# Graph network on one core: three spherical chunks copied over the rows by DMA, both small weight layers in fp32 on two row halves, edge features loaded once

## The reference, cut to what matters

```python
wk = relu(edge_features @ k_w1 + k_b1) @ k_w2 + k_b2      # [E, 128], the same with v_ for wv
acc = sh[:, 0:1] * (x_dst @ C[:, 0, :])                   # tensor_product: S = 9 spherical numbers
for s in range(1, S):
    acc = acc + sh[:, s:s+1] * (x_dst @ C[:, s, :])
k = (acc with Cqk) * wk                                   # and v = (acc with Cv) * wv
attn = einsum('ehd,ehd->eh', q[edge_src], k)              # then a softmax over the edges of a node
upd  = segment_sum(v * alpha)                             # and the weighted sum of the values
```

## Time and profile before

| | us |
|---|---|
| median of 3 runs | 2949.27 |
| profiled execution, its own time | 2947.53 |
| its span | 2945.7 |
| TensorE busy in the span | 2469.1 |
| VectorE | 2612.7 |
| GpSimd | 1731.3 |
| ScalarE | 1514.6 |

### The profile page before, as it was taken

One profiled execution on the slowest core, in us unless ns is written; L12 is line 12 of the kernel. 1 busy time (PEld: TensorE's weight loads), 2 busy tenths in 40 slices (PEclk: granted clock), 3 DMA queues, 4 the chain that ended last, 5 costly groups with the idle time before them and its releaser, 6 DMA issues.

```text
span 2945.7 us, 48186 instructions
## 1 busy us (share of the span) xinstructions
PE 2469.1 (84%) x12310; PEld 1787.3 (61%) x12505; DVE 2612.7 (89%) x3389; ACT 1514.6 (51%) x2914; POOL 1731.3 (59%) x1719
## 2 busy tenths in 40 slices
PE   2233347999999999999999999999999999999714
PEld 1233315677777776777677776777677777777511
DVE  6688835899999999999999999999999999999737
ACT  1321224566666655666566665666566566666310
POOL 1800037777777766667676666666666677665030
PEclk7555557999999999999999999999999999999855
DMA  6787714245555544444444444444445544544340
GB/s 187 202 222 187 210 25 111 76 131 149 148 149 145 148 147 139 141 142 148 139 144 142 146 147 140 140 144 147 142 141 147 148 141 142 148 144 132 121 124 11
DMA packets 282407, 415.35 MB, mean 141 GB/s; under 512 B 64463, under 2 KB 191875, under 8 KB 278470
## 3 DMA queue, kind: packets, MB, share of 16 engines
q1 hardware_dynamic: 222278, 296.67, 32.4%
q0 software_dynamic: 52704, 107.19, 15.1%
q10 hardware_dynamic: 7128, 8.13, 0.8%
HBM read 309.59 MB, written 102.20 MB: 140 GB/s over the span
## 4 chain that ended last, share of the span: by engine, by line
PE 52%; DVE 7%; issue 6%; ACT 3%; DMA 2%; POOL 2%; SPq 0%; DVEq 0%; ACTq 0%; POOLq 0%
PE bank L1118 11%; PE bank L1120 9%; PE bank L1119 9%; PE bank L1142 5%; PE bank L1163 4%; PE bank L1194 2%; PE bank L1124 2%; PE bank L1125 2%; PE bank L1095 2%; PE bank L1113 2%; DVE xa_t L1538 1%; DVE z_l L1546 1%; PE bank L1102 1%; POOL gathered L745 1%; PE bank L1101 1%
## 5 line engine op out<-in xcount | busy, mean ns | idle before, releaser
L745 POOL DMA_INDIRECT gathered<-xtab_d,src_g x784 | 780.6, 996 | 449.7 <-PE bank L1095 203.0
L745 POOL DMA_INDIRECT gathered<-qtab_d,dst_g x784 | 801.9, 1023 | 257.2 <-issue 249.0
L1118 PE MATMUL bank<-z_h,wt_h 128*128 128x512 f32 x1568 | 729.6, 465 | 27.9 <-DVE val L1578 27.9
L1538 DVE TENSOR_TENSOR xa_t<-bank,r_r 128x512 f32<-128x512 f32 x980 | 667.3, 683 | 13.5 <-PE bank L1142 10.3
L876 ACT ACTIVATE z_h<-xa_t 128x512 fp32r<-128x512 f32 x980 | 617.4, 634 | 110.1 <-DVE xa_t L1538 100.3
L1120 PE MATMUL bank<-z_h,wt_l 128*128 128x512 f32 x1568 | 620.7, 396 | 0.0
L1119 PE MATMUL bank<-z_l,wt_h 128*128 128x512 f32 x1568 | 618.8, 395 | 0.0
L1546 DVE TENSOR_TENSOR z_l<-xa_t,z_h 128x1024 fp32r<-128x1024 f32 x392 | 478.0, 1219 | 48.2 <-ACT z_h L876 44.6
L1118 PEld LDWEIGHTS bank<-z_h,wt_h 128*128 128x128 f32 x1568 | 301.1, 192 | 131.4 <-issue 92.7
L869 ACT ACTIVATE hid<-bank,b1kv 128x512 f32<-128x512 f32 x196 | 134.8, 688 | 476.4 <-PE bank L1102 462.4
L1120 PEld LDWEIGHTS bank<-z_h,wt_l 128*128 128x128 f32 x1568 | 294.9, 188 | 69.2
(11 more groups left out here) (222 smaller groups left out, 4057.9 us busy)
## 6 DMA issues: line engine op xcount, KB each, us to landing
nrow_d<-x_r SPq DMA_DIRECT2D x196, 288.0 KB
ea<-in_ea_t SPq DMA_DIRECT2D x392, 128.0 KB
exb<-exd_d SPq DMA_DIRECT2D x392, 128.0 KB
dmb<-exd_d SPq DMA_DIRECT2D x392, 128.0 KB
ea_c<-in_ea_t SPq DMA_DIRECT2D x49, 512.0 KB, 5.0
aggrow_d<-xa_t SPq DMA_DIRECT2D x49, 512.0 KB, 3.9
gathered<-xtab_d,src_g POOLq DMA_INDIRECT x784
gathered<-qtab_d,dst_g POOLq DMA_INDIRECT x784
```

Of the source, the lines that this page charges most:

```text
L745: rows_in = pool.indirect_dma_start(rows[:, c % 4, k, :], None, table, bass.IndirectOffsetOnAxis(ap=picked[:, s, at:at + 1], axis=0))
L1118: pe.matmul(ps[:, :], wt_h[rows, w, :], high, start=start, stop=False)
L1538: dve.tensor_tensor(z[:, i, :], bank[2 + (NJ * c + i) % 2][:, :], xt[:, c % 2, :], ALU.mult).then_inc(z_ok, 1)
```

## The change

Chunks 0 and 1 stay as they are (NS = 2); the numbers of chunks 2, 3 and 4 come straight from HBM in fp32 by three DMAs of a group, `load_harmonics`, with semaphores of their own (`sh_b_in`). VectorE multiplies these three chunks in one instruction, ScalarE rounds them in one, so `z_ok` counts NZ = 3 a group. Both small layers use plain fp32 matmuls without a split. The edge features of a group are loaded once: columns 0 to 255 on partitions 0 to 63 and 256 to 511 on 64 to 127. `hidden` has one matmul of 256 columns for each half, into banks 2 and 3; it is moved a group ahead and behind `weights`. `weights` has four of 256 columns, in turns on partitions 0 to 63 and 64 to 127.

```diff
             def load_edge(j, c):
-                past(sp, eal_ok, j, c, 2)
+                past(sp, hid_ps, j, c, 2, 2)
                 hold()
                 for half in range(2):
-                    sp.dma_start(ea2[half * D:(half + 1) * D, c % 2, :], edges_t[:, bass.ds(group(j, c) * G, G)]
-                                 ).then_inc(ea_in[c % 2], 16)
+                    sp.dma_start(ea2[half * D:(half + 1) * D, c % 2, :],
+                                 columns(edges_t, j, c)[:, half * HG:(half + 1) * HG]).then_inc(ea_in[c % 2], 16)
...
+            def load_harmonics(j, c):
+                past(sp, z_ok, j, c, 2, NZ)
+                hold()
+                for i in range(NS, NJ):
+                    k = 2 * i
+                    rows = columns(harmonics_t[k:min(k + 2, S), :], j, c)
+                    n = min(2, S - k)
+                    sp.dma_start(sh_b[:, c % 2, i - NS, :], rows.rearrange("s (o w) -> s o w", o=1)
+                                 .to_broadcast([n, P // n, G])).then_inc(sh_b_in[c % 2], 16)
...
             def body(j, c):
+                if live(j, c + 2):
+                    load_harmonics(j, c + 2)
                 if live(j, c + 3):
                     load_edge(j, c + 3)
...
             def front_h(j, c):
-                done(act, hid_ps, j, c)
+                done(act, hid_ps, j, c, 2)
+                past(act, wk_ps, j, c, 1)
                 past(act, wv_ps, j, c, 1)
-                act.activation(hid[:, :], ps_hw[:, :], ACT.Relu, bias=b1kv[:, :]).then_inc(hid_ok, 1)
-                act.activation(hid_h[:, :], ps_hw[:, :], ACT.Relu, bias=b1kv[:, :]).then_inc(hid_ok, 1)
+                for f in range(2):
+                    act.activation(hid[:, f * HG:(f + 1) * HG], bank[2 + f][:, 0:HG], ACT.Relu, bias=b1kv[:, :]
+                                   ).then_inc(hid_ok, 1)
...
             def hidden(j, c):
-                done(pe, eal_ok, j, c)
-                past(pe, wv_ok, j, c, 1)
-                pe.matmul(ps_hw[:, :], wt_h[:, W1KV, :], ea_hl[:, c % 2, :], start=True, stop=False)
-                pe.matmul(ps_hw[:, :], wt_l[:, W1KV, :], ea_hl[:, c % 2, :], start=False, stop=True
-                          ).then_inc(hid_ps, 1)
+                landed(pe, ea_in, j, c, 32)
+                if not isinstance(j, int) or c >= 1:
+                    done(pe, z_ok, j, c - 1, NZ, NS - NZ)
+                for f in range(2):
+                    half = slice(f * D, (f + 1) * D)
+                    pe.matmul(bank[2 + f][:, 0:HG], w1kv[half, :], ea2[half, c % 2, :], start=True, stop=True
+                              ).then_inc(hid_ps, 1)
...
-                for ps, rows, done_ps in ((ps_xw, slice(0, D), wk_ps), (ps_hw, slice(D, P), wv_ps)):
-                    split_matmul(ps, W2KV, hid_h[rows, :], hid_l[rows, :], True, True, rows).then_inc(done_ps, 1)
+                for f in range(2):
+                    edges = slice(f * HG, (f + 1) * HG)
+                    mk = pe.matmul(ps_xw[:, edges], w2kv[0:D, :], hid[0:D, edges], start=True, stop=True)
+                    mv = pe.matmul(ps_hw[:, edges], w2kv[D:P, :], hid[D:P, edges], start=True, stop=True)
+                mk.then_inc(wk_ps, 1)
+                mv.then_inc(wv_ps, 1)
...
             def outer(j, c, i):
...
+                if i < NS:
+                    done(dve, shb_ps, j, c, NS, i + 1 - NS)
+                    dve.tensor_tensor(z[:, i, :], bank[2 + i][:, :], xt[:, c % 2, :], ALU.mult).then_inc(z_ok, 1)
+                else:
+                    landed(dve, sh_b_in, j, c, 16 * (NJ - NS))
+                    dve.tensor_tensor(z[:, NS:NJ, :], sh_b[:, c % 2, :, :],
+                                      xt[:, c % 2, :].rearrange("p (o g) -> p o g", o=1)
+                                      .to_broadcast([P, NJ - NS, G]), ALU.mult).then_inc(z_ok, 1)
```

More of the change, by code:

```diff
@@ L27 @@
 NJ = 5
-CK, CV, W2KV, W1KV = 0, NJ, 2 * NJ, 2 * NJ + 1
-NW = 2 * NJ + 2
+CK, CV, CEND = 0, NJ, 2 * NJ
+NW = CEND
+NS = 2
+NZ = 3
 H = 8
@@ L102, in gnn_two_layers @@
         wt_l = sb("wt_l", [P, NW, O], F32R)
+        w1kv = sb("w1kv", [P, O])
+        w2kv = sb("w2kv", [P, O])
         head_sel = sb("head_sel", [P, 2 * BP - H])
@@ L350, in gnn_two_layers @@
         qg_in = [sem(f"qg_in{i}") for i in range(2)]
-        eah_ok = sem("eah_ok")
-        eal_ok = sem("eal_ok")
+        sh_b_in = [sem(f"sh_b_in{i}") for i in range(2)]
         batch_in = sem("batch_in")
@@ L507, in arrived, with columns, loads_and_stores @@
                 eng.wait_ge(ring[b], (g - b + n) * (per // n))
-        def loads_and_stores(sp, edges_t):
+        def columns(m, j, c):
+            turn, at = divmod(c, UNROLL)
+            by_turn = m.rearrange("d (n u w) -> d n u w", u=UNROLL, w=G)
+            if isinstance(j, int):
+                return by_turn[:, turn, at, :]
+            return by_turn[:, bass.ds(j + turn, 1), at, :].rearrange("d o w -> d (o w)")
+        def loads_and_stores(sp, edges_t, harmonics_t):
             sp.dma_start(x_r[:, :, 0:D], a["x"].rearrange("(t p) d -> p t d", p=P)).then_inc(x_in, 16)
@@ L590, in load_edge @@
                 hold()
-                sp.dma_start(s3[0:SP3, c % 4, :], sh3_d.rearrange("a s e -> (a s) e")[:, bass.ds(group(j, c) * G, G)]
-                             ).then_inc(s3_in[c % 2], 16)
+                sp.dma_start(s3[0:SP3, c % 4, :], columns(sh3_d.rearrange("a s e -> (a s) e"), j, c)).then_inc(s3_in[c % 2], 16)
+            def load_harmonics(j, c):
[7 more added lines that the diff above has]
+                                 .to_broadcast([n, P // n, G])).then_inc(sh_b_in[c % 2], 16)
             def store_exponents(j, s):
@@ L615, in store_row @@
                 hold()
-                sp.dma_start(nrow_d[bass.ds(group(j, c) * G, G), :].rearrange("(p j) w -> p (j w)", p=P),
+                turn, at = divmod(c, UNROLL)
+                to = nrow_d.rearrange("(n u p k) w -> n u p (k w)", u=UNROLL, p=P, k=4)
+                to = to[turn, at] if isinstance(j, int) else \
+                    to[bass.ds(j + turn, 1), at].rearrange("o p w -> (o p) w")
+                sp.dma_start(to,
                              row[:, c % 2, :, :].rearrange("p j w -> p (j w)")).then_inc(row_out[c % 2], 16)
             def body(j, c):
+                if live(j, c + 2):
+                    load_harmonics(j, c + 2)
                 if live(j, c + 3):
@@ L874, in outer_high @@
                     past(act, acc_ps, j, c, 2)
-                done(act, z_ok, j, c, NJ, i + 1 - NJ)
-                act.activation(z_h[:, c % 2, i, :], z[:, i, :], ACT.Copy).then_inc(zh_ok, 1)
+                done(act, z_ok, j, c, NZ, i + 1 - NZ)
+                chunks = slice(i, i + 1) if i < NS else slice(NS, NJ)
+                act.activation(z_h[:, c % 2, chunks, :], z[:, chunks, :], ACT.Copy).then_inc(zh_ok, 1)
             def front_q(j, c):
@@ L1083, in _ @@
             pe.wait_ge(sel_done, 1)
-            pe.wait_ge(wtl_padded, 3)
+            pe.wait_ge(wtl_padded, 2)
             pe.wait_ge(head_ok, 2)
@@ L1139, in spread @@
                     landed(pe, s3_in, j, c)
-                if not isinstance(j, int) or c * NJ + i >= 2:
-                    done(pe, z_ok, j, c, NJ, i - 1 - NJ)
-                pe.matmul(bank[2 + (NJ * c + i) % 2][:, :], sel[:, i, :], s3[:, c % 4, :], start=True, stop=True
-                          ).then_inc(shb_ps, 1)
+                    done(pe, hid_ok, j, c, 2)
+                pe.matmul(bank[2 + i][:, :], sel[:, i, :], s3[:, c % 4, :], start=True, stop=True).then_inc(shb_ps, 1)
             def products(j, c, i):
@@ L1199, in body @@
                 if live(j, c + 1):
-                    spread(j, c + 1, 0)
-                    spread(j, c + 1, 1)
+                    for i in range(NS):
+                        spread(j, c + 1, i)
                 if live(j, c + 2):
@@ L1206, in body @@
                 if live(j, c + 1):
-                    hidden(j, c + 1)
                     q_turn(j, c + 1)
@@ L1211, in body @@
                         products(j, c, i)
-                    if i + 2 < NJ and live(j, c + 1):
-                        spread(j, c + 1, i + 2)
                     if i == 1 and live(j, c + 1):
                         weights(j, c + 1)
+                    if i == 1 and live(j, c + 2):
+                        hidden(j, c + 2)
                     s = batch_at(c, 10)
@@ L1367, in _ @@
             dve.wait_ge(wtl_ok, 1)
-            for w in (CK + 4, CV + 4, W1KV):
+            for w in (CK + 4, CV + 4):
                 dve.memset(wt_l[D:P, w, :].bitcast(F32), 0.0).then_inc(wtl_padded, 1)
@@ L1628, in body @@
                     outer(j, c + 1, 1)
-                    hidden_low(j, c + 1)
+                    outer(j, c + 1, 2)
+                    outer_low(j, c + 1, 0)
                 if live(j, c - LAG):
                     sum_values(j, c - LAG)
-                if live(j, c + 1):
-                    outer_low(j, c + 1, 0)
-                    outer(j, c + 1, 2)
```

(6 more changed lines are left out.)

57 lines of the change are left out of this document (18 added, 39 removed).

## The result

The changed kernel takes 4099.07 us (median of 4 runs, 4096.1 to 4104.68) against 2949.32 (4 runs, 2947.16 to 2950.45) for the kernel before on the same chip: ratio 1.390, 95% interval 1.388 to 1.393. The forecast was 4130 us, slower.

What follows compares the result with a forecast made beforehand. It took two DMA engines, carrying the copies with two source rows, as the bound: 184 x 18.0 + 12 x 14.3 = 3484 us replaces the loop's 2300, so 2949 - 2300 + 3484 = 4133, about 4130 us; range 3800 to 4500.

Steps and rivals of the forecast that it cites:

- Two engines for a pair copy, 18.0 us a group: Copies of chunks 2 and 3: two source rows mean two DMA engines, 408 KB each, 18.0 us a group.
- The sum: Whole kernel: 184 groups at 18.0 us and 12 at 14.3 make 3484 us for 2300, rest unchanged, 4133 us.
- VectorE waits at the product of three chunks, some 7 us a group: Sign on VectorE: it would wait for a DMA at the three-chunk product, some 7 us a group.
- DMA share some 0.4: Sign in the profile: share falls to some 0.4 though bytes rise by nearly two fifths, as most engines idle.
- The exponents' copies queue behind: DMA queue: the exponents' copies would wait behind the copies on the two engines, which need 11.5 us a group.
- Issuing them is no matter: SyncE's queue: issuing the three added DMAs takes 0.63 us each, 1.9 us more a body, and doesn't matter.
- Passes side by side, 1.58 us for the added block; TensorE 10.85 us: TensorE: six fp32 half-row matmuls in three slots of 0.43 plus 0.29, 1.58 us; body 11.43 - 2.16 + 1.58 = 10.85.
- Clock mixed, TensorE within the 18 us: TensorE's clock: expected mixed, its work still inside 18 us a group; the clock as the bound had 0.03.
- VectorE's work, 10.0 us a group: VectorE: from 11.3 us a group, less two dropped instructions and some 0.1 from the fused product, to 10.0.
- By the row GpSimd stays at 10.1 us: GpSimd's gathers: unslowed beside VectorE instructions with two SBUF inputs, 10.1 us a group; by the skill's rule up to 11.9.
- the wide rival: DMA copies spread over eight or more engines: TensorE sets the pace, 10.9 us a group, 2800 us; chance 0.09.
- the other side of the forecast: Whole kernel faster, about 2800 us, if the copies spread wide; faster by over 0.2% had chance 0.09.

Runs made afterwards that it cites:

- e1_wide: The changed kernel with each copy of chunks 2 and 3 cut into two DMAs of one source row, same bytes: 3096.66 us, ratio 1.050.
- e9_six: e1_wide with three gathers where four are, TensorE turning the third tile twice: 2789.54 us, ratio 0.947.
- e7_weights: The kernel before with only the second small layer in plain fp32, four matmuls of 256 columns on two row halves: 2959.92 us, ratio 1.005.
- e5_thirds: e1_wide with the three-chunk product cut into three one-chunk instructions that follow each other at the same place: 2925.57 us, ratio 0.992.
- e11_cuts: e5_thirds with the two z_l instructions of 1024 columns cut into four of 512: 2844.89 us, ratio 0.965.
- e2_half: The changed kernel with the copy of chunk 2 alone cut into two DMAs of one source row: 3274.92 us, ratio 1.112.
- e3_four: The changed kernel with chunks 2 and 3 each copied from four source rows to 32 partitions: 3177.76 us (one run).

## Why the prediction was right, and where it was not

- **Two engines for a pair copy, 18.0 us a group.** Right, the mechanism too: 17.8 us once exponents and rows are there, and 14.1 for the twelve groups before, where the sum had 18.0 and 14.3. By the 408 KB of the busiest engine that is 408 / 17.8 = 22.9 KB/us, where I took 22.8 from the best slice. Two engines show in the DMA share of 0.13, in the increments that come late and in their number. `e1_wide` shows that it is the shape of the copy and not its bytes: 1002 us less with the same bytes.
- **The sum.** The loop came out at 3421 us and not 3484, 63 less; what lies outside it came out at 4099 - 3421 = 678 us and not 649, 29 more, of which 17 lie ahead of the first spread (476.5 for 459.4 us). The sum took this part as unchanged, and why it grew wasn't followed. The two misses partly cancel, so that 4133 stands as near to 4099 as it does is in part luck.
- **VectorE waits at the product of three chunks, some 7 us a group.** Right, 6.7. **DMA share some 0.4.** Right, 0.42.
- **The exponents' copies queue behind.** Right in kind: what lies behind the pair copies on the two engines is late. The page of waits shows it at the edge features, for which TensorE waits 4.4 us a group. "Issuing them is no matter" was wrong: three issues took 9.35 us. No run shows that this cost time of its own, and none rules it out; the 18.0 us of the two engines account for the whole without it.
- **Passes side by side, 1.58 us for the added block; TensorE 10.85 us.** Right: 1.59 us for the block and 10.88 us a body in `e9_six`, 1.15 for the four matmuls of `weights` alone in `e7_weights`.
- **Clock mixed, TensorE within the 18 us.** Right: 0.83 granted, with TensorE busy 225 of 300 us.
- **VectorE's work, 10.0 us a group.** Near: 269 of 300 us in `e9_six`, 9.8 a group. Three products of 682 ns against one of 1756 are 0.29 us less by these rows, not the 0.1 of the text; nothing hangs on it.
- **The step that failed: "By the row GpSimd stays at 10.1 us".** In the earlier trace rows the gather had begun 0.16 us before the VectorE instruction, so it wasn't the one to wait. The rows of `e1_wide` with the other order show the hold, and so do rows of the kernel before. Worked out from `e1_wide`, gathers cost (1.24 - 1.00) x 8 = 1.9 us more a group, close to the "up to 1.8" that I wrote down from the Trainium skill's rule (GPSIMD Engine Reference, 8. Key points) and then set aside. In the changed kernel this lies under the copies' 17.8 us and costs nothing; but the wide rival was priced at 2800 us, and with the change as written it is 3097. So the other side of the forecast, faster with 0.09, needed more than wide copies: it needed the product cut as well (`e5_thirds`, `e11_cuts`).

What stays open: what part of `e2_half` and `e3_four` beyond the count of engines belongs to the held gathers; what the stopped queue costs by itself; and why the part outside the loop grew by 29 us.

## What to carry to other kernels

Before a DMA that fans a few rows out to many partitions, count its source rows: with two of them a copy ran on two of 16 engines, and the same bytes as two DMAs of one row each took a quarter off the kernel's time. A DMA share that falls while the bytes rise is how it looks in a profile, and two increments of another DMA that come late, behind 14 in time, show it directly. Where GpSimd's instructions stand near the bound, the length of VectorE's instructions with two SBUF inputs counts, not only their sum, and so does when the others begin: with one product of three chunks the kernel took 171 us more than with three products, though the fused one saves VectorE 0.14 us a group (1.75 against 1.89). A row that shows two instructions side by side says nothing of a hold until one has looked at which began first.

## What the runs showed of the hardware

- A copy of two source rows to 128 partitions ran on two DMA engines: share 0.13 at 49 GB/s, and 3 semaphore increments. Four rows made 5, eight rows 9 and one row 16.
- While those two engines were behind, the issue of three copies held SyncE's queue for 9.35 us (0.63 us an issue in the kernel before, 0.50 in `e1_wide`). Two of the 16 parts of each load of edge features came late, up to 10.3 us after the issue, where in `e1_wide` all had come after 4.3.
- A gather that began while a VectorE `tensor_tensor` with two SBUF inputs ran ended 0.82 us after that instruction (217 of 232 in a millisecond of `e1_wide` within 0.80 to 0.83), and one that began in a scan some 0.75 us after it. One that began 0.16 us before the instruction kept its 0.94 us; from 0 to 0.06 us before it both happen: 23 such gathers of `e9_six` were held, for 2.09 us, and others were not.
- 768 KB a group more on the DMA engines, spread wide, cost nothing while GpSimd set the pace: 3096.66 us with them and 3099.45 without, at a DMA share of 0.67 and 0.42.
